# Two batches' convolution parts, one after the other or one slot apart: attention, then deformable convolutions on one core

## What is computed

```python
# layer 0: group norm, 4-head attention over the 4096 pixels, projection
x = xn + proj(softmax(q k / 8) v)
# layer 1: a position term is added
# layer 2: 1x1 convolution to 64 channels, relu (h)
off = conv3x3(h, woff) + boff                    # 27 channels: 18 offsets, 9 masks
samp = bilinear(h, y, x) * mask                  # 4 corners, 9 taps per pixel
x = relu(bn(conv1x1(relu(bn(einsum('bckhw,ock->bohw', samp, w2))), w3)) + x)
# layer 3: twice (layer = 0, 1): relu(group norm), then
f = depthwise conv7x3 ... off = conv1x1(f)       # 7x7 depthwise, 18 offsets
sampled = bilinear_gather(h, py, px)             # 4 corners, 9 taps, 256 channels
h = einsum('bckhw,ock->bohw', sampled, w) + b
# the result is h + x
```

## Time and profile before

| | |
|---|---|
| median of 3 runs | 5940.25 us (5938.71 to 5950.32) |
| profiled execution | 5940.5 us, its span 5938.7 us |
| PE busy | 5171.5 us (87%) |
| DVE busy | 4237.4 us (71%) |
| ACT busy | 2202.9 us (37%) |
| POOL busy | 3186.0 us (54%) |
| mean granted PE clock | 0.932 of 2.4 GHz |
| DMA | 790.65 MB, mean 133 GB/s |

### The profile page before, as it was taken

How to read it: one execution, slowest core, us unless ns; L and a number is a source line. 1 busy time by engine, 2 the same in 40 slices (tenths; PEclk the granted TensorE clock), 3 DMA queues, 4 the chain that set the end, 5 groups by cost and what they waited for, 6 DMA issues and landing times. The chain is left out here.

```text
span 5938.7 us, 76314 instructions
## 1 busy us (share of the span) xinstructions
PE 5171.5 (87%) x23148; PEld 2417.5 (41%) x23148; DVE 4237.4 (71%) x6851; ACT 2202.9 (37%) x4004; POOL 3186.0 (54%) x2832
## 2 busy tenths in 40 slices
PE   7999999998676798878889999999986767888788
PEld 3333333333565344434433333333335753444344
DVE  5888888873223599579858888888732235995798
ACT  2444444441011156235524444444410111562355
POOL 0666666661773277157606666666617732771576
PEclk9999999998787899989999999999977878999899
DMA  1000000001333599579900000000013335995799
GB/s 55 1 1 1 1 1 1 1 1 33 98 105 112 196 409 410 190 284 410 366 29 1 1 1 1 1 1 1 1 33 100 105 111 195 409 410 192 283 410 367
DMA packets 310974, 790.65 MB, mean 133 GB/s; under 512 B 69512, under 2 KB 136401, under 8 KB 310222
## 3 DMA queue, kind: packets, MB, share of 16 engines
q0 software_dynamic: 193536, 679.59, 29.9%
q1 hardware_dynamic: 117198, 107.99, 6.0%
HBM read 701.57 MB, written 85.87 MB: 133 GB/s over the span
## 5 line engine op out<-in xcount | busy, mean ns | idle before, releaser
L580 POOL TENSOR_TENSOR arena<-arena 128x512 f32<-128x512 f32 x960 | 1405.9, 1464 | 829.9 <-ACT arena L1056 765.7
L663 POOL DMA_INDIRECT arena<-corners,arena x1152 | 1083.7, 941 | 957.2 <-POOLq L658 577.9
L1056 ACT ACTIVATE arena<-ps 128x1024 f32<-128x1024 f32 x1024 | 1048.7, 1024 | 1239.8 <-PE ps L787 1210.0
L1472 DVE TENSOR_REDUCE arena<-ps 128x2 f32<-128x1024 f32 x1024 | 1243.3, 1214 | 347.1 <-PE ps L761 346.8
L990 PE MATMUL ps<-arena 128*128 128x512 f32 x2304 | 1054.6, 602 | 0.0
L787 PE MATMUL ps<-arena 64*128 64x512 f32 x4096 | 1046.5, 590 | 0.0
L1654 DVE SCALAR_TENSOR_TENSOR ps<-arena,ps 128x256 f32<-128x256 f32 x2304 | 957.2, 484 | 107.3 <-DVEq L1648 64.9
L800 PE MATMUL ps<-arena 128*64 128x512 f32 x4096 | 991.6, 605 | 0.0
L1494 DVE TENSOR_TENSOR arena<-arena 128x512 f32<-128x512 f32 x960 | 890.1, 927 | 62.5 <-ACT arena L1056 62.1
L1186 ACT ACTIVATE ps<-arena 128x256 f32<-128x256 f32 x1152 | 503.0, 468 | 662.0 <-DMA arena<-corners,arena 515.5
L617 POOL DMA_INDIRECT arena<-corners,arena x576 | 544.9, 946 | 353.8 <-issue 247.3
(11 more groups left out here) (129 smaller groups left out, 3420.9 us busy)
## 6 DMA issues: line engine op xcount, KB each, us to landing
corners<-arena SPq DMA_DIRECT2D x256, 256.0 KB, 3.9
arena<-corners,arena POOLq DMA_INDIRECT x1728, 8.0
arena<-in_wd SPq DMA_DIRECT2D x4, 2304.0 KB, 8.2
X<-in_x SPq DMA_DIRECT2D x8, 1024.0 KB, 8.4
corners<-arena SPq DMA_DIRECT2D x128, 64.0 KB, 2.2
out_y<-arena SPq DMA_DIRECT2D x32, 256.0 KB, 6.1
arena<-in_base SPq DMA_DIRECT2D x4, 288.0 KB, 9.2
arena<-in_base SPq DMA_DIRECT2D x2, 432.0 KB, 3.2
```

The source lines that it names most:

```text
L580: pool.tensor_tensor(SUMS[u % 2][:, 0, :], SUMS[u % 2][:, 0, :], P[n % 4][:, 0, :], ALU.add).then_inc(sum_a, 1)
L663: pool.indirect_dma_start(G3[4 * k + t].rearrange("p a c -> p (a c)"), None, table256, bass.IndirectOffsetOnAxis(ap=IS3[:, k, t:t + 1], ax ...
L1056: af(P[n % 4].rearrange("p h q -> p (h q)"), ps[:, 2 * (n % 2):2 * (n % 2) + 2, :].rearrange("p h q -> p (h q)"), ACT.Exp, scale=float(D) ...
L1472: v.tensor_reduce(mxp[i % 2][:, :, j], ps[:, 4:6, :], AX.X, ALU.max).then_inc(mx_done, 1)
```

## The change

Both attentions now come first. Behind the first one X is written to DRAM (`between`), quarter by quarter as its projection ends, and the x of batch 1 is loaded in its place. Then the rest runs for both batches in one list of stages, batch 1 a slot ahead. Each slot holds the gathers and sums of one batch and, beside them, the table and the offset convolution of the other:

| gathers and sums | beside them |
|---|---|
| (none) | table and offsets, 64 channels, batch 1 |
| 64 channels, batch 1 | table and offsets, 64 channels, batch 0 |
| 64 channels, batch 0 | table and offsets, 256 channels, layer 0, batch 1 |
| 256 channels, layer 0, batch 1 | the same, layer 0, batch 0 |
| 256 channels, layer 0, batch 0 | layer 1, batch 1 |
| 256 channels, layer 1, batch 1 | layer 1, batch 0 |
| 256 channels, layer 1, batch 0 | (none) |

Between the slots stand relu, `corners` of one batch and the group norm of the other. The side work is written by hand into each engine's order (`beside`), a piece after or before a tile or tap. It has one bank of PSUM for the kernel rows (4) and one for all else (5), which is handed on by `side_bank`; one buffer for the shifts, and one staging tile TS3 (or TS2[0]) for the table's writes, whose freeing (`ts_free0`) ACT waits for. ACT takes the transposes out of PSUM, where DVE did. In layer 2's sums the fifth block of `summed` moves to bank 1 and has one buffer where there were two. Each batch has its own tables in DRAM and its own image in SBUF, 70 rows high, in which the normalized image is written in place; so the input of layer 3 is kept in DRAM (`resid`) and fetched before layer 1's sums. The border rows of four tables are written where there were two, and the start no longer waits for them.

```diff
-        table64 = nc.dram_tensor("corners64", (TY * TY, 4 * CB), F32, kind="Internal").ap()
-        table256 = nc.dram_tensor("corners256", (TY * TY, 4 * C), F32, kind="Internal").ap()
-
-
-        X = sb("X", [128, CH, PIX])
+        table64 = [nc.dram_tensor(f"corners64_{b}", (TY * TY, 4 * CB), F32, kind="Internal").ap() for b in range(B)]
+        table256 = [nc.dram_tensor(f"corners256_{b}", (TY * TY, 4 * C), F32, kind="Internal").ap() for b in range(B)]
+        between = nc.dram_tensor("between", (128, CH, PIX), F32, kind="Internal").ap()
+        resid = [nc.dram_tensor(f"resid{b}", (128, CH, PIX), F32, kind="Internal").ap() for b in range(B)]
+
+
+        img1 = sb("img1", [128, CH, ROWS7 * W])
+        X = img1[:, :, 3 * W:3 * W + PIX]
...
+                if b == 0:
+                    for i in range(4):
+                        at = slice(i * PIX // 4, (i + 1) * PIX // 4)
+                        sp.wait_ge(projected, 2 * CH * (i + 1))
+                        sp.dma_start(between[:, :, at], X[:, :, at]).then_inc(spilled[i], 16)
+                    for i in range(4):
+                        at = slice(i * PIX // 4, (i + 1) * PIX // 4)
+                        sp.wait_ge(spilled[i], 16)
+                        sp.sem_inc(spilled[i], -16)
+                        sp.dma_start(X[:, :, at], x[1:2, :, at].rearrange("o (a p) n -> p (o a) n", p=128)).then_inc(x_part[i], 16)
...
+            def keep_residual(b):
+
+                sp.wait_ge(relu_done, 2)
+                for i in range(4):
+                    at = slice(i * PIX // 4, (i + 1) * PIX // 4)
+                    sp.dma_start(resid[b][:, :, at], INNER[b][:, :, at]).then_inc(spilled[i], 16)
...
+            table_writes(0, 0, TS3, table256[0], C)
+            with sp.Fori(0, NCH - 1) as g:
+                table_writes(0, g + 1, TS3, table256[0], C)
+                group_done(1, g)
+            group_done(1, NCH - 1)
...
+            def side_shifted(tbuf, ksize, no, sel):
+
+                pe.wait_ge(side_bank, 1)
+                pe.sem_inc(side_bank, -1)
+                for t in range(4):
+                    last = mm(ps[:, 5, t * no:(t + 1) * no], tbuf[:, t * 128:(t + 1) * 128],
+                              sel[:, ksize:ksize + no], start=True, stop=True)
+                last.then_inc(off_ready, 1)
...
+            def side_table3(part):
+
+                if part == 0:
+                    pe.wait_ge(stage_ready, CH)
+                    pe.sem_inc(stage_ready, -CH)
+                pe.wait_ge(side_bank, 1)
+                pe.sem_inc(side_bank, -1)
+                for t in range(2):
+                    at = (2 * part + t) * 128
...
+                        last = tr(ps[:, 5, t * C + half * 128:t * C + (half + 1) * 128],
+                                  NS3[:, half, at:at + 128], ident_s[:, :])
+                last.then_inc(side_ps, 1)
+
+            def side_rows3(b, n, some):
+
+                for i in some:
+                    half, ky = i // 7, i % 7
+                    last = mm(ps[0:7 * O3, 4, :], WO[:, half, ky, :], IMG[b][:, half, bass.ds((8 * n + ky) * W, CHUNK)],
+                              start=(i == 0), stop=(i == 13))
+                    if i == 13:
...
+                def beside(n, q, first, ahead, last):
+
+                    if side == 64:
+                        if q == 0 and not last:
+                            side_table2()
+                        if q == 1 and ahead:
+                            side_conv1(n + 2)
+                        if q == 2:
+                            if not first:
+                                side_shifts_done()
+                                side_shifted(T2[0], 3, O2, sel2_s)
+                            side_rows2(n)
+                    else:
+                        if q < 2 and not last:
+                            side_table3(q)
+                        if q == 2 and not first:
+                            side_shifts_done()
+                            side_shifted(T3[0], 7, O3, sel3_s)
+                        if q >= 2:
+                            side_rows3(1, n, range(7 * (q - 2), 7 * (q - 1)))
+
...
+                def beside(n, k, first, last):
+
+                    if k < 2 and not last:
+                        side_table3(k)
+                    if k == 2 and not first:
+                        side_shifts_done()
+                    if k == 4 and not first:
+                        side_shifted(T3[0], 7, O3, sel3_s)
+                    if k >= 2:
+                        side_rows3(side, n, range(2 * (k - 2), 2 * (k - 1)))
...
+            def side_normal(b, n, half):
+
+                at = chunk(n)
+                af(NS3[:, half, :], INNER[b][:, half, at], ACT.Relu,
+                   scale=gsc[:, half:half + 1], bias=gbi[:, half:half + 1])
+                af(INNER[b][:, half, at], INNER[b][:, half, at], ACT.Relu,
+                   scale=gsc[:, half:half + 1], bias=gbi[:, half:half + 1]).then_inc(stage_ready, 1)
+
+            def side_copy(to, width, begins, ends):
+
+                act.wait_ge(side_ps, 1)
+                act.sem_inc(side_ps, -1)
+                if begins:
+                    act.wait_ge(ts_free0, 16 * 8)
+                    act.sem_inc(ts_free0, -16 * 8)
+                af(to.rearrange("p a b -> p (a b)"), ps[:, 5, 0:width], ACT.Copy).then_inc(side_copied, 1)
+                act.wait_ge(side_copied, 1)
+                act.sem_inc(side_copied, -1)
+                act.sem_inc(side_bank, 1)
+                if ends:
+                    act.sem_inc(ts_ready, 1)
+
...
+                def beside(n, k, ahead, last):
+
+                    if 2 <= k <= 3 and not last:
+                        side_copy3(k - 2)
+                    if 5 <= k <= 6 and ahead:
+                        side_normal(side, n + 2, k - 5)
+
+                def nine(g, first=False, ahead=True, last=False):
+
+                    for k in range(KK):
+                        products(3 * g + k // 3, k % 3)
+                        if k > 0 or not first:
+                            staged((k - 1) % 3)
+                        if k == 1 and not first and layer == 0:
+                            output(g - 1)
...
+                def nine(g, first=False):
+
+                    for k in range(KK):
+                        sampled(k % 3, 0)
+                        if k == 1 and not first and layer == 1:
+                            output(g - 1)
+                        sampled(k % 3, 1)
+                        if side is not None and not first:
+                            if k == 1:
+                                side_shifts3()
+                            if k == 7:
+                                side_offsets3(g - 1)
...
+            table_and_offsets(TS2, ps[:, 1, 0:4 * CB], OFF2, BASE2, 3, T2, sel2_s, O2)
+
+            meet()
+            corners64()
+
+            meet()
+            sums64(1, 0, 64)
+
+            meet()
+            relu_half(1)
+            corners64()
+            dve.wait_ge(relu_done, 2)
+            group_norm(INNER[1], GN1_G, GN1_B)
+            offset_weights(0)
+            bias_base(BASE3, pwb_s[:, 0, :])
+
+            meet()
+            sums64(0, 1, 256)
+
+            meet()
+            relu_half(0)
+            corners256()
+            dve.wait_ge(relu_done, 2)
+            group_norm(INNER[0], GN1_G, GN1_B)
+
+            meet()
+            sums256(1, 0, 0)
+
+            meet()
+            corners256()
+            group_norm(INNER[1], GN2_G, GN2_B)
+            offset_weights(1)
+            bias_base(BASE3, pwb_s[:, 1, :])
+
+            meet()
+            sums256(0, 0, 1)
+
+            meet()
+            corners256()
+            group_norm(INNER[0], GN2_G, GN2_B)
+
+            meet()
+            sums256(1, 1, 0)
+
+            meet()
+            corners256()
+
+            meet()
+            sums256(0, 1, None)
+
+            meet()
 
 
 def constants():
```

More of the change, by code:

```diff
@@ L863, in _, with meet @@
                 pe.sem_inc(go_pe, -1)
+            def meet():
                 pe.drain().then_inc(arrived, 1)
@@ new lines, in four @@
+                def four(n, first=False, ahead=True, last=False):
+                    for q in range(4):
+                        beside(n, q, first, ahead, last)
+                        if not (last and q == 3):
+                            summed(4 * n + q + 1, (q + 1) % 4)
+                        else:
+                            staged_sums()
+                        mixed(q % 2)
+                if side == 64:
+                    side_conv1(0)
+                    side_table2()
+                    side_conv1(1)
+                else:
+                    side_table3(0)
+                    side_table3(1)
@@ L1018, in _ @@
+            products256(None)
+            meet()
         @block.scalar
@@ new lines, in four @@
+                def four(n, ahead=True, last=False):
+                    for q in range(4):
+                        if not (last and q == 3):
```

(15 more changed lines are left out.)

1169 lines of the change are left out of this document (621 added, 548 removed).

## The result

The changed kernel takes 5,706.97 us (median; 5,704.12 to 5,712.10), the kernel before 5,945.18 us: a ratio of 0.9603, 95% interval 0.9591 to 0.9614. The forecast was 5,690 us (5,580 to 5,830).

What follows compares the result with a forecast made beforehand. The prediction took DMA to bound the 256-channel gathers and POOL's issuing the 64-channel ones, with table stages as serial time. Gains of 68 + 104 + 80 + 0 + 0 = 252 us from 5940.5 gave 5,690 us (5,580 to 5,830).

Steps and rivals of the forecast that it cites:

- A beside B: 64-channel table and offset convolution (A) beside other batch's 64-channel gathers and sums (B): 8 us growth, gain 68 us.
- C beside B: 256-channel table and offset convolution (C) beside 64-channel gathers and sums (B): PE 46.7 us a group, gain 104 us.
- C beside D, layer 0: 256-channel table (C) beside 256-channel gathers and sums (D), twice: PE becomes the bound, 56 us a group, gain 40 each.
- C beside D, layer 1: 256-channel table (C) beside layer 1's gathers (D): DVE's wait for PE's last tap gives 61.8 us a group, gain about 0.
- What moves: Relu, normalization, corners, spills, fetches and border DMAs in other places: taken as 0 us (-15 to +15).
- What would show it: Signs expected in the profile: stage lengths, POOL issuing without pause, PE over 97% busy in layer 0, idle in layer 1.
- Rival 1: 256-channel gather stages: DMA and PE overlap badly and add up, 65 us a group; 5,780 to 5,925 us, chance 0.17.
- Rival 2: PE gains more: full clock in 64-channel gathers, no waits in 256-channel ones; 5,560 to 5,610 us, chance 0.12.
- Rival 3: ACT waits for single stage buffer TS3; slower if a table DMA takes over 7.5 us; over 5,952 us, chance 0.06.
- Rival 4: No overlap: the batches' steps wait on each other in engine order, nothing won, 5,940 us; chance 0.03.

Runs made afterwards that it cites:

- few products: Changed kernel with 2 of 14 offset-convolution products a group in second B and second D (other edits elsewhere): second B 395.7 us for 409.3, second D 52.8 us a group for 54.8.
- output through ACT: Changed kernel, but ACT takes layer 1's output from PSUM at tap 1 and DVE adds the residual at tap 5: 5,655.58 us, 0.9518 of the kernel before.
- The kernel without writes in its second D: Changed kernel, second D with no table writes and 2 of 14 offset-convolution products, other edits elsewhere: 49.8 us a group there for 54.8, stage 420 us.
- double writes: Changed kernel with a second set of 64 table writes to a scratch tensor: first D 55.8 us a group for 54.8; in another kernel third D 62.3 for 62.2.

## Right and wrong, step by step

The prediction was right in sign, in size and in where most of the time goes. That the total came within 20 us is in part luck: errors of some 54 us stand on one side of its sum and of 35 on the other.

*A beside B*: forecast 8 us of growth, measured 12.7 with the pace at POOL's 45. Only the opening and closing chain was too small.

*C beside B*: forecast 14 us from a pace of 46.7 and 5 for opening and tail, measured 27.9 in all. The pace failed: it was 45.3. Of the two corrections that the prediction set against each other, both held, the clock at 1.00 in the steady groups (40.7 us busy, not 46.7) and the four waits of 0.9 us, and together they give 44.3 us, not 46.7. That few products brought back 13.6 us, as if the 14 had been right, is a coincidence: what they removed was the lag of the opening.

*C beside D, layer 0*: 56 us a group were forecast, 54.8 measured: PE busy 52.9 and idle 1.9, where 53.9 and 2 were said. The taps were over-counted, not the side work. In these rows (PE, output through ACT, third D) a tap takes 5051.48 - 5047.16 = 4.32 us, not 4.46, since its eight transposes come in one piece; the two side products behind it take 1.71, 12.0 for all 14:

```profile
5047.16 1.04 PE L1135 MATMUL ps<-ident_s,arena 128*128 128x128 f32 x8
5048.04 3.60 PE L1145 MATMUL ps<-arena 128*128 128x512 f32 x8
5051.48 1.88 PE L1034 MATMUL ps<-arena 128*126 x4
5053.19 1.04 PE L1135 MATMUL ps<-ident_s,arena 128*128 128x128 f32 x8
```

That is 8 x 1.2 = 10 us in the kernel's favour. But opening and tail grew by 87.4 - 8 x (54.8 - 46.3) = 19 us, not 5. About 9 of them lie behind the last sum, where the last shifts and offsets stand alone. Most of the others are the wait for the stage buffer at the opening. The kernel without writes in its second D shows what it costs: ACT's wait there shrinks to the one for PE's transposes (ACT's waits, 4225 to 4665 us),

```profile
ACT arena L1376 <- ACTq L1375: 1.6, 1, 1.6
```

and the sums take 395.3 us, 3 less than eight groups of 49.8; in the kernel with few products and all writes they take 428.9, 6.5 more than eight of 52.8. So the wait is worth some 10 us there, and the other two D have one as long.

*C beside D, layer 1*: 61.8 us a group were forecast, 62.2 measured. The order of events was right, 2.62 us of idle at tap 1 for the 2.7 forecast and 4.8 at tap 2 for 5.2 in the group shown, 6.8 a group in the mean. What was missed is that PE, after such a stop, runs its next products at the lower clock, 6.00 us for 3.60, 2.8 us a group by the busy times above; against it stand the over-counted taps and 1.1 us less of idle. Two more terms were wrong: the growth was counted from 46.3 us a group, which is layer 0's, where a layer-1 D took 378.9 / 8 = 47.4 before, and nothing was set for opening and tail, which took some 15 us. So the stage grew by 133 us, not 124, and laying C beside it lost 10 us.

*What moves*: taken as 0, it came to about 15 us of gain. The traces show where most of it lies: the second batch's A had taken 81.6 us before (4366.0 to 4447.7), not 76, and the one that stays took less than the first of before, 6 us together; the stretches between the stages and the `corners` add up to 11 us less; the two attentions and what stands around them to 3 more. Why each differs was not looked into.

*The lengths in "What would show it"* were short: 460, 460, 505 and 380 us were forecast for the four D, 476, 477, 533 and 401 measured. They were counted from the windows of the earlier trace rows, 365 and 379 us, which leave out the stages' ends (381.4 and 388.9), and a layer-1 D was taken as long as a layer-0 one (399.3).

*The rivals.* Rival 1 (65 us a group) is refuted by the double writes. Rival 2 asked for no waits in D; the version with the output through ACT is that case for layer 1. Rival 3 needed a table DMA of over 7.5 us, eight of them 60; they took 30 at the opening. In the steady groups the buffer is never waited for, and even with twice the writes in the first D its pace was 55.8; but once a D, at the opening, its mechanism is at work, as told above, and the prediction had set nothing for that. The Trainium skill (same page, "Queues, rings and completion order") has each engine take its queues in turn, a packet at a time; the trace agrees in so far as the writes landed while gathers kept the engines full, though in 30 us for eight, where one took 3.9 in a stage without gathers. Rival 4 is out by the first table above.

What would have corrected the sum: 5 + 9 + 14 + 14 = 42 us more of growth over the two B and the two layer-0 D, 10 more in layer 1 and 2 in the last D, against which stand 2 x 10 us from the 1.2 us a group, and the 15 us of what moves: 252 - 42 - 10 - 2 + 20 + 15 = 233, measured 232.8.

*What stays open*: what stops PE for 2 to 11 us in the gather stages of the first two chips; why the parts of what moves differ; and what a second stage buffer would bring (some 30 us by the three waits, an estimate: no run has one).

## To carry over

Two stages laid beside each other cost the largest of their summed demands per engine, not their sum, but each new pairing pays an opening and a closing of its own, 13 to 26 us here; count it for every stage. A buffer that is never waited for in the steady groups can still stop everything at the opening, where two groups follow each other closely (10 us here). An engine that must wait for the bound engine's last result just before it feeds that engine again hands its whole wait on to it: let an engine with slack take the result out (53 us here), and don't expect the same where another resource is the bound. Here the load of the table writes came out right by their bytes at the rate reached beside the gathers (5.1 us a group), not by the packet time that they showed alone (7.1).

## What was not expected of the hardware

- Eight products of 128x512 took 6.00 us after stops of 3.10 and 1.70 us and 3.60 us otherwise. Around them the granted clock was 0.69 (5107 to 5118 us; 0.50 from 5111 to 5114), and 1.00 in the 7 us before and the 12 us behind. In the steady piece of the third D its mean was 0.95, in the one without the stops 1.00, so short stops of PE were followed by stretches at 1.2 of 2.4 GHz.
- Gathers and table writes together ran at 412 GB/s, as fast as gathers alone (410). But eight writes of 256 KB took 30 us beside the gathers, from the first issue to a free buffer, where one took 3.9 us to land in the table stage of before.
- The kernel before took 5,941 and 5,945 us on two chips and 6,720 and 6,724 us on two others, where the changed kernel's variants had every gather stage, B and D, stretched by 90 to 150 us, and PE's signal in the row shown 7.6 us behind the modelled end of its products.
